# A two-layer graph network on one core: TensorE's order of the second layer, with the next batch's features turned in the batch before

## What is computed

```python
R = relu(abs_distances[:, None] @ w1 + b1) @ w2 + b2
Y = spherical_harmonics(rel_vec)
Fj = features[src]
...
        acc = acc + _NORM[i] * jnp.einsum('euv,ef,evi,ofi->euo', Rb[..., k], Yf, Fb, C)
...
out = out.at[dst].add(msg)
```

## Time and profile before

| | us |
|---|---|
| median of 3 runs | 3802.88 |
| lowest and highest run | 3799.03, 3805.24 |
| the profiled execution | 3798.03 |
| its span, first to last instruction | 3796.3 |
| layer 0 and the nodes behind it | to about 1595 |
| layer 1, its 98 batches | about 1595 to 3660 |
| the nodes at the end | about 3660 to 3796 |

### The profile page before, as it was taken

One profiled execution on the slowest core, in us unless ns is written; L12 is line 12 of the kernel. 1 busy time (PEld: TensorE's weight loads), 2 busy tenths in 40 slices (PEclk: granted clock), 3 DMA queues, 4 the chain that ended last, 5 costly groups with the idle time before them and its releaser, 6 DMA issues.

```text
span 3796.3 us, 58108 instructions
## 1 busy us (share of the span) xinstructions
PE 3310.6 (87%) x17312; PEld 1902.1 (50%) x17312; DVE 2762.8 (73%) x3470; ACT 2061.5 (54%) x2391; POOL 2786.3 (73%) x2915
## 2 busy tenths in 40 slices
PE   4999999999999883399999999999999999999963
PEld 3898889898989783222323232333323232323232
DVE  5787877787878785467777777777777777777765
ACT  4777777776777660145454545454554545454520
POOL 6777777777777776677777777777777777777746
PEclk9999999999999995599999999999999999999975
DMA  4122222222122211122222222222222222222211
GB/s 100 39 57 41 52 43 43 50 44 54 40 55 43 50 48 29 39 57 53 62 55 59 55 59 55 59 58 56 62 52 62 55 59 54 59 55 59 57 28 26
DMA packets 188428, 197.65 MB, mean 52 GB/s; under 512 B 60241, under 2 KB 149427, under 8 KB 188085
## 3 DMA queue, kind: packets, MB, share of 16 engines
q1 hardware_dynamic: 95508, 149.13, 13.7%
q0 software_dynamic: 92832, 47.72, 9.7%
HBM read 134.02 MB, written 62.59 MB: 52 GB/s over the span
## 4 chain that ended last, share of the span: by engine, by line
PE 70%; ACT 12%; DVE 5%; POOL 5%; issue 5%; DMA 1%; SPq 0%; ACTq 0%; DVEq 0%; POOLq 0%
PE ps_r L940 19%; PE ps_r L990 17%; PE ps_m L1027 10%; PE ps_m L940 10%; PE ps_r L1018 8%; ACT prod_room L822 8%; POOL ngot L667 4%; DVE unit L1645 3%; PE ps_m L1037 2%; PE ps_r L1002 2%; ACT f_across L829 2%; PE ps_r L924 1%; ACT hot_s L739 1%; PE ps_m L1043 1%; ACT hot_s L742 1%
## 5 line engine op out<-in xcount | busy, mean ns | idle before, releaser
L688 POOL DMA_INDIRECT got<-x_d,idx x1564 | 1506.2, 963 | 530.6 <-issue 504.7
L822 ACT ACTIVATE prod_room<-ps_r,bias_col 128x1024 f32<-128x1024 f32 x392 | 435.9, 1112 | 780.0 <-PE ps_r L990 531.9
L940 PE MATMUL ps_r<-x_hi,hot_s 128*128 128x448 f32 x1974 | 741.6, 376 | 41.7 <-ACT hot_s L742 41.7
L1645 DVE TENSOR_TENSOR x_room<-radial_more,ps_r 128x1024 f32<-128x1024 f32 x392 | 475.0, 1212 | 384.0 <-PE ps_r L1018 252.3
L990 PE MATMUL ps_r<-hid,wc 64*128 64x512 f32 (+1 forms) x2352 | 669.8, 646 | 81.2 <-ACT prod_room L822 72.9
L940 PE MATMUL ps_r<-x_lo,hot_s 128*128 128x448 f32 x1974 | 733.0, 371 | 0.0
L739 ACT ACTIVATE hot_s<-rows,minus_row 128x512 fp32r<-128x512 f16 (+1 forms) x658 | 449.0, 764 | 244.0 <-PE ps_m L940 206.2
L1018 PE MATMUL ps_r<-ft,repeat 32*128 32x512 f32 (+1 forms) x2352 | 553.4, 639 | 1.1 <-ACT ft L848 0.6
L1645 DVE TENSOR_TENSOR unit<-prod_room,ps_r 128x1024 f32<-128x1024 f32 x392 | 451.1, 1213 | 106.9 <-PE ps_r L1018 102.0
L940 PEld LDWEIGHTS ps_r<-x_hi,hot_s 128*128 128x128 f32 x1974 | 378.3, 192 | 75.5 <-issue 43.0
L990 PEld LDWEIGHTS ps_r<-hid,wc 64*128 64x128 f32 x2352 | 178.8, 186 | 448.8 <-ACT prod_room L822 255.3
(11 more groups left out here) (203 smaller groups left out, 4438.4 us busy)
## 6 DMA issues: line engine op xcount, KB each, us to landing
hid<-weight_t SPq DMA_DIRECT2D x196, 256.0 KB
run_d<-runs_t SPq DMA_DIRECT2D x194, 256.0 KB
got<-x_d,idx POOLq DMA_INDIRECT x1564
rows<-code_d SPq DMA_DIRECT2D x47, 160.0 KB
frame_d<-x_sb SPq DMA_DIRECT2D x7, 1008.0 KB, 4.5
frame<-frame_d SPq DMA_DIRECT2D x98, 72.0 KB
frame_b<-frame_d SPq DMA_DIRECT2D x98, 72.0 KB
rows<-code_d SPq DMA_DIRECT2D x47, 128.0 KB
```

Of the source, the lines that this page charges most:

```text
L688: pool.indirect_dma_start(got[k][:, t, :], None, x1_d, bass.IndirectOffsetOnAxis(ap=idx[k][:, t:t + 1], axis=0)).then_inc(got2_landed[k], 16)
L822: act.activation(radial_s[u][:, :, 0:w], radial_slot[:, :, 0:w], ACT.Identity, bias=bias_col[:, c:c + 1]).then_inc(radial_copied, 1)
L940: mm = pe.matmul(found[BANK_OF[k][g]], hot_s[k][:, a, g, :], part[:, a * LN * D:(a + 1) * LN * D], start=(a == 0 and n == 0), stop=(a == B ...
L1645: dve.tensor_tensor(product[q][h][:, :, 0:w], radial_s[u][:, :, 0:w], spread_slot[(k + s_ + 1) % 2][:, :, 0:w], ALU.mult).then_inc(multipl ...
```

## The change

Layer 1's order is rewritten on PE, ACT and DVE:

- TF of the next batch stands at the end of a batch, between R4 and R5, and writes into the bank of the messages (`turned_p`), not into a spread slot. ACT copies the scalars of the next batch behind its copy of R4, then the indices, then the turned features (into one of two buffers `ft`), and then copies R5.
- PE's order in a batch: S0, SP3 of the batch before, S1, its TM, S2, R0 (of the next batch), AA of the batch before, R1, SP0, S3, SP1, R2, S4, S5, SP2, R3, R4, TF (next batch), R5.
- On ACT, the copy of R3 moves behind the turn of the sums and the ReLU.
- DVE's rotation (now `rotate`) is that of the next batch, between m5 and m6; the turning back stands behind m1, the scan behind m4.
- The radial copies of R4 and R5 get a second pair of rooms, the spreads take slots by their own number alone, and the waits follow from that.

The diff, cut to the orders and the functions that they call:

```diff
-            def copy_radial(b, u, w=QUAD * P):
+            def copy_radial(b, k, u, w=QUAD * P):
 
                 c, h = RADIAL_UNITS[u]
                 act.wait_ge(radial_ready, UNITS * b + u + 1)
-                if not isinstance(b, int) or b > 0:
-                    act.wait_ge(multiplied, len(PRODUCTS) * (b - 1) + (1, 2, 3, 4, 7, 8)[u])
-                act.activation(radial_s[u][:, :, 0:w], radial_slot[:, :, 0:w], ACT.Identity,
...
+            def copy_scalars(b, k, rounds, n):
+
+                act.wait_ge(got2_landed[k], 16 * (T * rounds + n))
+                if not isinstance(b, int) or b > 1:
+                    act.wait_ge(turned, b - 1)
+                act.copy(turned_in[k][:, 0:n, 0:MUL], got[k][:, 0:n, 0:MUL]).then_inc(f0_copied, 1)
+
+            def copy_turned(b, k, w=QUAD * P):
+
+                act.wait_ge(turned, b + 1)
+                if not isinstance(b, int) or b > 1:
+                    act.wait_ge(spread_ready, UNITS * (b - 1))
+                act.copy(ft[k][:, 0:w], turned_p[:, 0:w]).then_inc(ft_ready, 1)
+
             def layer1(i, last=False):
                 for k in range(2):
                     b = 2 * i + k
                     first, final = isinstance(b, int) and b == 0, last and k == 1
-                    n = TL if final else T
-                    w = TL // QUAD * P if final else QUAD * P
+                    n = TL if last else T
+                    w = n // QUAD * P
                     if not first:
                         copy_summed(b - 1)
-                    act.wait_ge(got2_landed[k], 16 * (T * i + n))
-                    if not isinstance(b, int) or b > 1:
-                        act.wait_ge(turned, b - 1)
-                    act.copy(turned_in[k][:, 0:n, 0:MUL], got[k][:, 0:n, 0:MUL]).then_inc(f0_copied, 1)
-                    copy_radial(b, UNITS - 1, w)
-                    act.copy(idx[k][:, :], src_all[:, bass.ds((b + 2) * T, T)]).then_inc(idx_ready, 1)
-                    act.wait_ge(turned, b + 1)
-                    if not first:
-                        act.wait_ge(spread_ready, UNITS * b)
-                    act.copy(ft[:, 0:w], spread_slot[k][:, 0, 0:w]).then_inc(ft_ready, 1)
-                    if not first:
                         masks2(b - 1, 1 - k)
                     if not final:
-                        later = TL // QUAD * P if last else QUAD * P
-                        for u in range(4):
-                            copy_radial(b + 1, u, later)
+                        for u in range(3):
+                            copy_radial(b + 1, 1 - k, u, w)
                     if not first:
                         carry_and_turn(b - 1, 1 - k)
                     if not last:
                         relu(k, i + 2)
                     if not final:
-                        copy_radial(b + 1, 4, later)
+                        copy_radial(b + 1, 1 - k, 3, w)
+                        copy_radial(b + 1, 1 - k, 4, w)
+                        copy_scalars(b + 1, 1 - k, i + k, n)
+                        if not last:
+                            act.copy(idx[1 - k][:, :], src_all[:, bass.ds((b + 3) * T, T)]).then_inc(idx_ready, 1)
+                        copy_turned(b + 1, 1 - k, w)
+                        copy_radial(b + 1, 1 - k, 5, w)
...
                 pe.wait_ge(f0_copied, b + 1)
-                if not isinstance(b, int) or b > 0:
-                    pe.wait_ge(multiplied, len(PRODUCTS) * b - 1)
+                if not isinstance(b, int) or b > 1:
+                    pe.wait_ge(scanned, BATCHES + b - 1)
                 for j in range(w // P):
-                    mm = pe.transpose(spread_slot[k][:, 0, j * P:(j + 1) * P],
+                    mm = pe.transpose(turned_p[:, j * P:(j + 1) * P],
                                       turned_in[k][:, QUAD * j:QUAD * (j + 1), :].rearrange("p t f -> p (t f)"), ident[:, :])
                 mm.then_inc(turned, 1)
 
             def spread_features(b, k, s, w=QUAD * P):
 
                 c, h = SPREADS[s]
-                slot = spread_slot[(k + s + 1) % 2]
+                slot = spread_slot[s % 2]
                 if s == 0:
                     pe.wait_ge(ft_ready, b + 1)
-                    if not isinstance(b, int) or b > 0:
-                        pe.wait_ge(multiplied, len(PRODUCTS) * b)
+                if s < 2 and (not isinstance(b, int) or b > 0):
+                    pe.wait_ge(multiplied, len(PRODUCTS) * (b - 1) + s + 7)
                 if s > 1:
                     pe.wait_ge(multiplied, len(PRODUCTS) * b + (2, 4, 5, 6)[s - 2])
                 for t in range(2):
                     group = slice((2 * h + t) * D, (2 * h + t + 1) * D)
-                    mm = pe.matmul(slot[:, t, 0:w], repeat[group, c, :], ft[group, 0:w], start=True, stop=True)
+                    mm = pe.matmul(slot[:, t, 0:w], repeat[group, c, :], ft[k][group, 0:w], start=True, stop=True)
...
+                    spread_features(b, k, 0, w)
                     if not first:
                         sum_products(b - 1, 3)
+                    spread_features(b, k, 1, w)
+                    if not first:
                         turn_messages(b - 1)
-                    turn_features(b, k, w)
+                    spread_features(b, k, 2, w)
                     if not final:
                         radial(b + 1, 1 - k, 0, later)
-                    spread_features(b, k, 0, w)
-                    spread_features(b, k, 1, w)
                     if not first:
                         add_axes(b - 1)
                     if not final:
                         radial(b + 1, 1 - k, 1, later)
-                    spread_features(b, k, 2, w)
                     sum_products(b, 0, w)
+                    spread_features(b, k, 3, w)
                     sum_products(b, 1, w)
                     if not final:
                         radial(b + 1, 1 - k, 2, later)
-                    spread_features(b, k, 3, w)
-                    if not final:
-                        radial(b + 1, 1 - k, 3, later)
                     spread_features(b, k, 4, w)
-                    if not final:
-                        radial(b + 1, 1 - k, 4, later)
                     spread_features(b, k, 5, w)
                     sum_products(b, 2, w)
                     if not final:
+                        radial(b + 1, 1 - k, 3, later)
+                        radial(b + 1, 1 - k, 4, later)
+                        turn_features(b + 1, 1 - k, later)
                         radial(b + 1, 1 - k, 5, later)
...
+            def rotate(b, k, rounds, n=T):
+
+                dve.wait_ge(got2_landed[k], 16 * (T * rounds + n))
+                dve.wait_ge(frame_loaded[k], 16 * (rounds + 1))
+                f1 = got[k][:, 0:n, MUL:D].rearrange("p t (v c) -> p t v c", c=3)
+                for c in range(3):
+                    s.mark(dve.tensor_tensor(part[:, c, 0:n], spread(f1[:, :, :, c], 2, 3),
+                                             spread(frame[k][:, 0:n, c, :], 3, MUL), ALU.mult))
+                s.settle()
+                s.mark(dve.tensor_tensor(part[:, 0, 0:n], part[:, 0, 0:n], part[:, 1, 0:n], ALU.add))
+                s.settle()
+                if not isinstance(b, int) or b > 1:
+                    dve.wait_ge(turned, b - 1)
+                dve.tensor_tensor(turned_in[k][:, 0:n, MUL:D], part[:, 0, 0:n].rearrange("p t i v -> p t (i v)"),
+                                  part[:, 2, 0:n].rearrange("p t i v -> p t (i v)"), ALU.add).then_inc(rotated_in, 1)
 
             def layer1(i, first, last=False):
                 for k in range(2):
                     b = 2 * i + k
-                    short = last and k == 1
-                    n = TL if short else T
-                    w = n // QUAD * P
-
-                    dve.wait_ge(got2_landed[k], 16 * (T * i + n))
-                    dve.wait_ge(frame_loaded[k], 16 * (i + 1))
-                    f1 = got[k][:, 0:n, MUL:D].rearrange("p t (v c) -> p t v c", c=3)
-                    for c in range(3):
-                        s.mark(dve.tensor_tensor(part[:, c, 0:n], spread(f1[:, :, :, c], 2, 3),
-                                                 spread(frame[k][:, 0:n, c, :], 3, MUL), ALU.mult))
-                    s.settle()
-                    s.mark(dve.tensor_tensor(part[:, 0, 0:n], part[:, 0, 0:n], part[:, 1, 0:n], ALU.add))
-                    s.settle()
-                    if not isinstance(b, int) or b > 1:
-                        dve.wait_ge(turned, b - 1)
-                    dve.tensor_tensor(turned_in[k][:, 0:n, MUL:D], part[:, 0, 0:n].rearrange("p t i v -> p t (i v)"),
-                                      part[:, 2, 0:n].rearrange("p t i v -> p t (i v)"), ALU.add).then_inc(rotated_in, 1)
-                    if not (first and k == 0):
+                    begun = not (first and k == 0)
+                    final = last and k == 1
+                    w = (TL if final else T) // QUAD * P
+                    multiply(b, k, 0, w)
```

(52 more changed lines are left out.)

6 lines of the change are left out of this document (3 added, 3 removed).

## The result

The changed kernel takes 4108.0 us (median of four runs) against 3800.95 us for the kernel before (four runs): 1.08 times, with a 95% interval of 1.0776 to 1.0823. One of the four took 5198.34 us at a granted clock of 0.63 over its span, against 4098.82 to 4109.15 at 0.91 for the three others, from which the ratio comes; no trace of it was kept. The kernel is slower by 307 us; the forecast was 4039, its range 3910 to 4115. The profiled execution took 4098.82 us, its span is 4097.1.

What follows compares the result with a forecast made beforehand. PE was taken as the bound, POOL's gathers near it at 20.5 us a batch; 3798.0 (profiled run) + 127 (new order) + 109 (clock falls) + 4.9 (to the median) = 4039 us, range 3910 to 4115.

Steps and rivals of the forecast that it cites:

- The old waits: PE's four waits in a layer 1 batch, ahead of R1, R3, R4 and the turned messages: 1.75 us together, gone.
- the walk: Step-by-step timing of a layer 1 batch in the new order: 22.24 us against 20.93, +1.3 a batch, +127 us.
- S4 and S5 side by side: On PE, both spreads run together in 1.07 us, giving back the 1.06 lost by parting S0 and S1.
- The second rival: DVE's product m5 comes late, S4 and S5 run one behind the other: +102 us, 4030 with clock up; chance 0.07.
- The two new waits: PE at the batch's end: R4 idles 1.37 us for R3's copy, turned features 1.6 for the scalars' copy; +3.0 together.
- R5 hides the copy of the turned features: At the batch's end the copy is done at 21.9, under R5; without that cover S0 would wait 0.7 us.
- POOL, SP and DVE cost nothing: POOL's gathers and DVE's moved rotation add nothing in layer 1; SP's later loads nothing, at worst some tenths.
- the third rival: The radial and copy chain is covered, old waits go, POOL's 20.5 us a batch is the floor: 3761; chance 0.04.
- The clock falls, at 1.7 us: Idles between R3 and the turned features drop PE's clock; each fall costs 0.95 to 2.9 us, taken as 1.7.
- How often: Share of layer 1 batches with a clock fall: two in three taken, 64 x 1.7 = +109 us.
- The first rival: PE's clock holds in layer 1, so only the new order's +127 us counts: 3930; chance 0.25.
- The Trainium skill: Guide page cited against this order: short idles between matmul groups, from cycling PSUM slots, can make PE's clock swing.

Runs made afterwards that it cites:

- the two runs where they came in every third batch or more often: Both against the changed kernel: turned features moved behind R5, 4309.31 us; one unneeded 256-column matmul added just ahead of R3, 4446.3 us.

## Why the prediction was right, point by point

- **The old waits go.** Right: none is left ahead of TM, R1 or R3, and none came ahead of AA. S1 covers the copy of the sums, as the walk had it.
- **S4 and S5 side by side.** Right: 2526.92 - 2525.85 = 1.07 us for both, so S0 and S1 apart cost nothing in the sum. The second rival falls.
- **The two new waits.** Right in place and cause: 2.42 us from R3 to R4 (walk: 2.43), TF 2.80 behind R4 (2.67 in the walk; 2.65 where the clock is up). With the clock held, a batch is 22.13 us, 1.27 more than before; the walk said 22.24 and 1.31 (the parts that the prediction names for it, -1.75, +3.0 and +0.15, make 1.4; the sum goes by the walk).
- **R5 hides the copy of the turned features.** Right: S0 has no wait in the change, and 0.77 us where TF is last.
- **POOL, SP and DVE cost nothing.** Right; no wait of PE names them in layer 1. That POOL's 20.5 us is the floor under this order was the third rival's number, and the two runs with the radial units apart showed it.
- **The clock falls, at 1.7 us.** Right in kind: it falls behind these idles, and the filled idles show that it was the clock. The price, 1.75 us a batch, lies inside the 0.95 to 2.9 of the prediction; that it came so close to 1.7 is luck, as no row gave that figure, and a long fall costs some 8 us. The change had one long fall, near its start; in the two runs where they came in every third batch or more often the time was 4309 and 4446, above the range.
- **How often** is the term that was mis-sized: two batches in three were taken, 109 us; it is practically each batch, 168 us. With the other terms the sum is 3798.0 + 122 (walk, 127 in the prediction) + 168 + 11.8 (ahead of the first turned messages) - 1.2 (behind the last) + 9.2 (profiled execution to median, 4.9 in the prediction) = 4108. The 11.8 had no term in the prediction.
- **The first rival**, a clock that holds, would have given 3930; the run with filled idles gave 3927.92. That the two agree within 2 us is in part luck, since the walk was 5 us high and the late start is not in it.
- **The Trainium skill.** The sentence that rested on it ("TensorE: Matmul & The Clock Gate", section "A second HAM failure mode: psum-queue depth-cycling") agrees with this trace in that short idles make the clock swing, here between 1.00 and 0.50 in 95 of 97 batches. Only the first of the two idles is the PSUM slot's; the second comes from ACT's order.
- **The reason given for two in three** ("lies on the falling side") did not carry a share. Rows that show one fall tell that a gap can do it, not how often; the honest reading was the range from none to all, and the range held for that reason, by 7 us.

## What to carry to other kernels

Steps that pass one buffer to another engine and back need other work between them: three in a row cost the round trip each (2.42 us here), however busy the engine looks elsewhere, and a copy put behind one of them on the other engine waits with it. Price idles on TensorE twice, by their length and by what the clock takes behind them; here the clock took 1.75 us a batch, more than the 1.27 that the new order costs with the clock held. An order can be tested for that by filling the idles with work nobody needs: if the kernel gets faster, the clock was part of the loss.

## What was not expected of the hardware

- Idles of 1.29 and 1.67 us with one unit of 1.13 us between them brought the clock to 0.50 at the end of 95 of 97 batches. Single idles: 1.29 us did not, 1.52 in 9 of 97, 2.4 to 2.55 in 10 of 13. 1.50 and 0.71, with R4 and TF between them, did not.
- A fall can last: with PE busy 13.00 of 13.00 us the clock stayed at 0.50, where in the change it was mostly back within TF, R5 and S0. The long falls came in a rhythm of batches; what sets it is open.
- Time and work did not go together: 0.63 us more work a batch cost 3.5 us a batch in one place, and some 2 us more work a batch in the idles saved 1.75.
